# Causal attention on one core: the fourfold copy of v is dropped, and v is turned by products with the unit matrix

## The reference

```
t = t + attention(layer_norm(t))
Q = n @ W_Q;  K = n @ W_K;  V = n @ W_V        # n = layer_norm(t)
scores = Q K^T / sqrt(32), masked to key <= query
out = softmax(scores) V
```

## Time and profile before

| | us |
|---|---|
| median of three runs | 5225.98 |
| profiled execution | 5203.04 |
| its span in the trace | 5201.3 |

### The profile page before, as it was taken

The page is one execution under the profiler, slowest core; times in us unless marked ns, Lnnn a source line. Parts: engine busy times, 40 slices in busy tenths (PEclk is TensorE's granted clock), DMA queues, the critical chain, the costliest instruction groups (busy, mean ns, idle before and its releaser), DMA issues. The chain is left out here.

```text
span 5201.3 us, 102304 instructions
## 1 busy us (share of the span) xinstructions
PE 4473.6 (86%) x39002; PEld 2775.7 (53%) x39002; DVE 3218.9 (62%) x6562; ACT 2836.1 (55%) x5790; POOL 1475.1 (28%) x2257
## 2 busy tenths in 40 slices
PE   4888888886754899999999997679999999999955
PEld 2666666665322455555555554555555555555544
DVE  4777777776796466666666564336666666666532
ACT  2766676665654356555555554315555555655521
POOL 3111111111354333334243322023333243333100
PEclk8998999988877799999999998769999999999966
DMA  1100000000000000000000000000000000000003
GB/s 26 27 2 2 2 2 2 2 2 3 1 1 0 1 2 2 2 2 2 2 2 2 2 2 5 1 1 2 2 2 2 2 2 2 2 2 2 2 5 49
DMA packets 348174, 22.44 MB, mean 4 GB/s; under 512 B 346388, under 2 KB 347700, under 8 KB 347700
## 3 DMA queue, kind: packets, MB, share of 16 engines
q1 hardware_dynamic: 347700, 16.03, 4.2%
HBM read 7.88 MB, written 6.42 MB: 3 GB/s over the span
## 5 line engine op out<-in xcount | busy, mean ns | idle before, releaser
L551 DVE TENSOR_REDUCE L2a_mx<-L2a_r 128x1 f32<-128x512 f32 (+4 forms) x1344 | 771.0, 627 | 334.2 <-PE L2a_r L415 326.8
L551 DVE TENSOR_REDUCE L3a_mx<-L3a_r 128x1 f32<-128x512 f32 (+4 forms) x1344 | 770.8, 627 | 331.3 <-PE L3a_r L415 323.7
L415 PE MATMUL L2a_r<-L2a_vT,L2a_qT 32*128 32x512 f32 (+3 forms) x3488 | 885.5, 529 | 13.2 <-DVE L2a_mx L551 12.5
L415 PE MATMUL L3a_r<-L3a_vT,L3a_qT 32*128 32x512 f32 (+3 forms) x3488 | 881.8, 527 | 12.9 <-DVE L3a_mx L551 12.3
L514 ACT ACTIVATE L2a_e<-L2a_r 128x512 f32<-128x512 f32 (+3 forms) x1344 | 669.1, 569 | 266.8 <-PE L2a_r L394 263.3
L514 ACT ACTIVATE L3a_e<-L3a_r 128x512 f32<-128x512 f32 (+3 forms) x1344 | 669.0, 569 | 266.7 <-PE L3a_r L394 263.2
L394 PE MATMUL L2a_r<-L2a_qT,L2a_vT 32*128 32x512 f32 (+4 forms) x3488 | 772.4, 513 | 2.8 <-DMA L2a_qT<-L2a_nm 2.7
L394 PE MATMUL L3a_r<-L3a_qT,L3a_vT 32*128 32x512 f32 (+4 forms) x3488 | 770.8, 511 | 3.8 <-DMA L3a_qT<-L3a_nm 3.8
L415 PEld LDWEIGHTS L2a_r<-L2a_vT,L2a_qT 32*128 32x128 f32 x3488 | 387.4, 190 | 158.5 <-DVE L2a_mx L551 90.1
L415 PEld LDWEIGHTS L3a_r<-L3a_vT,L3a_qT 32*128 32x128 f32 x3488 | 385.8, 189 | 156.7 <-DVE L3a_mx L551 89.8
L1471 POOL TENSOR_SCALAR win_xw<-win_xr,win_rs,win_sh 32x343 f32<-32x343 f32 (+7 forms) x432 | 186.5, 446 | 937.0 <-DVE win_sh L1340 936.9
(11 more groups left out here) (376 smaller groups left out, 7573.8 us busy)
## 6 DMA issues: line engine op xcount, KB each, us to landing
L2a_qT<-L2a_nm SPq DMA_DIRECT2D x768, 0.5 KB, 2.0
L3a_qT<-L3a_nm SPq DMA_DIRECT2D x768, 0.5 KB, 2.0
T<-in_x SPq DMA_DIRECT2D x16, 384.0 KB, 3.8
out<-T SPq DMA_DIRECT2D x16, 384.0 KB, 4.0
win_mq<-win_nmt SPq DMA_DIRECT2D x256, 3.1 KB, 1.7
win_msk<-in_L_conv_pos_emb SPq DMA_DIRECT2D x49, 0.2 KB
L2a_qT<-L2a_nm SPq DMA_DIRECT2D x32, 0.2 KB, 1.8
L3a_qT<-L3a_nm SPq DMA_DIRECT2D x32, 0.2 KB, 1.8
```

The source lines that it names most:

```text
L415: return nc.tensor.matmul(bank_of(x)[:, o:o + c1 - c0], QT_[g0:g0 + C, img % 2, q0:q0 + P], VT[g0:g0 + C, img % 2, c0:c1], start=start, st ...
L551: return nc.vector.tensor_reduce(to, frm, AX.X, ALU.max)
```

## The change

`VR`, its memset, the item "vr" and the semaphore `vr_ready` are gone. The item vT now waits for `v_ready` and makes four products per tile: the weights are the 32 channels of the tile in `V`, the moving operand is the unit matrix, and product g writes partitions 32g to 32g + 31 of the bank. The due times of the vT items are moved within the image before. In the sorted list the seven vT items of an image were at the pv batches of slots 5, 15, 15, 26, 41, 50 and 60; now they are at 15, 26, 33, 41, 50, 50 and 60. Item v keeps its due time, and its rank is again the last.

```
-    RANK = {..., "out": 11, "vr": 12, "v": 13}
+    RANK = {..., "out": 11, "v": 12}
...
-            at = (img - 1) * PER + (4, 12, 20, 28, 38, 48, 58)[f]
+            at = (img - 1) * PER + (18, 24, 30, 38, 46, 54, 64)[f]
...
-        timed += [(vr - 19, ("res", img)), (vr - 7, ("rs", img)), (vr, ("vr", img)), (v, ("v", img))]
+        timed += [(vr - 19, ("res", img)), (vr - 7, ("rs", img)), (v, ("v", img))]
...
-        VR = sb("vr", [P, NT, QT, C])
...
-                nc.vector.memset(VR[:, :, :, 0:1], 1.0)
...
-                    elif kind == "vr":
+                    elif kind == "v":
                         img = x[1]
                         pool.wait_ge(root_ready, ROOT[("rs", img)] + 1)
-                        if img:
-                            pool.wait_ge(item_full, FILLED[("vT", img - 1, NJ - 1)] + 1)
-                        nc.gpsimd.tensor_tensor(
-                            VR[:, :, :, 1:C], RES[:, :, None, 1:C].to_broadcast([P, NT, QT, C - 1]),
-                            RSTD[:, img % 2][:, :, None, None].to_broadcast([P, NT, QT, C - 1]),
-                            ALU.mult).then_inc(vr_ready, 1)
-                    elif kind == "v":
-                        img = x[1]
                         if img > 1:
                             pool.wait_ge(pv_done, score_at(img - 1, 0))
...
                         if f == 0:
-                            pe.wait_ge(vr_ready, img + 1)
+                            pe.wait_ge(v_ready, img + 1)
                         for i in range(q_tiles(f)):
                             t = QT * f + i
                             r = rows(t)
-                            last = nc.tensor.transpose(bank_of(x)[:, i * P:i * P + r],
-                                                       VR[0:r, t].rearrange("p a c -> p (a c)"), k.ident[0:r, 0:r])
+                            for g in range(4):
+                                last = nc.tensor.matmul(bank_of(x)[g * C:(g + 1) * C, i * P:i * P + r],
+                                                        V[0:r, img % 2, t, :], k.ident[0:r, 0:r],
+                                                        start=True, stop=True)
```

More of the change, by code:

```diff
@@ L146, in causal_attention @@
             MAXES += [(img, j, x) for x in banks]
-    RANK = {"max": 1, "score": 0, "q": 2, "pv": 3, "acc": 4, "final": 5, "vT": 6, "mask": 7, "rs": 8, "ors": 9, "res": 10, "out": 11, "vr": 12, "v": 13}
+    RANK = {"max": 1, "score": 0, "q": 2, "pv": 3, "acc": 4, "final": 5, "vT": 6, "mask": 7, "rs": 8, "ors": 9, "res": 10, "out": 11, "v": 12}
     timed = [(n, ("score", n)) for n in range(NS)]
@@ L263, in _ @@
                 nc.vector.memset(O0[:], 0.0)
-        vr_ready, v_ready = sem("vr_ready"), sem("v_ready")
+        v_ready = sem("v_ready")
         stat_step, var_ready, log_ready, root_ready = sem("stat_step"), sem("var_ready"), sem("log_ready"), sem("root_ready")
```

## The result

The changed kernel takes 5405.36 us (median of four runs, 5390.51 to 5409.18) against 5222.56 us for the kernel before, run beside it (four runs, 5218.76 to 5230.42). The ratio is 1.0355, with a 95% interval of 1.0337 to 1.0373, so 183 us more. The forecast was 180 us more, 5406 us. The total fits better than its terms do; the experiments show that their errors cancel.

A forecast was written before the change was run, and what follows sets the result against it. TensorE was taken to bound the kernel. Products 67, wait for v 79, clock falls 44 and layer start -10 us summed to +180 on 5226, giving 5406 us, range 5325 to 5500.

The forecast's parts named there:

- What bounds the kernel: In pv phases TensorE sets the pace, busy 86% of the span; work added there delays everybody behind it.
- A: vT on TensorE, images 1 to 15 of both layers: products cost more than transposes, 67 us (32 to 224).
- D: Start of each layer: earlier first vT and no first-pv gap, against slower image 0 products; net -10 us in all.
- The factor of four: Rival on vT: transposes four times faster than float32 products, so products cost 273 us, in all 5612 us; chance 0.03.
- The rival of column tiles not side by side: On vT: a tile's products take 0.432 us, so products cost 224 us, in all 5563 us; chance 0.07.
- B: First vT of images from 2 on: TensorE waits 2.82 us for GpSimd's v in 28 places, 79 us.
- C: Behind the wait for v: TensorE's clock falls nearly each time, 28 x 1.56 = 44 us (0 to 73).
- the new due times: vT items move from slots 5 and 15 to 33 and 50, one starved phase to another; costed at nothing.
- more falls at block 0: With the vT gone from slot 5, the clock may fall at block 0 in the other images too, 23 us more.
- The rival on the other side: Seven banks between TensorE and VectorE/ScalarE hide added time and wait; only layer starts remain: 5207 us, chance 0.04.

The follow-up runs named there:

- doubled products: Changed kernel with v ranked before final, each tile's four products issued twice, against the kernel before: 5414.55 us, ratio 1.0380.
- products alone: Kernel before, keeping copy and old due times, each transpose replaced by four products with the unit matrix: 5306.12 us, ratio 1.0174.
- v ahead of final: Changed kernel with only v's rank edited, so GpSimd writes v before adding block 0's result: 5261.94 us, 1.0088 of the kernel before.
- the kernel with the clock held: Changed kernel in which TensorE fills its wait for v with twelve bf16 products: 5340.7 us, 1.0225 of the kernel before.
- the late copy: Kernel before with copy and v of image 1 due three slots later: 5206.71 us, ratio 0.9979; with new vT due times too, 5189.07 us, 0.9945.
- the new times alone: Kernel before with the new due times of vT and nothing else: 5200.73 us against 5211.81, ratio 0.9977.

## Why the prediction was right

**What bounds the kernel: right.** Each microsecond added to TensorE in a pv phase came back in the time: products, doubled products and the wait all did (the wait 2.72 of its 2.75 us, the second set of products 5.35 us per image).

**A, the products: right in kind, too small.** The term was 67 us, and the 4.5 us per layer for image 0 in D belong to it, 76 together. The products alone cost 91 us (79 to 102 by the interval). The step that was off is the duration of a group, 0.86 us by the first eight records of a pv. A single group takes 1.02 us and two together 1.88, so the places of an image take 6.2 us in the changed kernel against 3.2 with transposes, 3.0 us more where 2.2 was forecast; the distances without falls say 3.15 for the two shown (93.93 against 90.77) and 3.0 in the mean. The price of more records was right: a second set of 32 makes a single group 0.87 us longer, 0.109 us per four records, and 5.35 us per image. So the missing time belongs to the group and not to the records, and I had no row for that. The factor of four in the Trainium skill ("TensorE: Matmul & The Clock Gate", section Terms) asked for 273 us. This case's trace does not agree with it: products and transposes of an image stand at 6.2 to 3.2 us, a factor of 1.9. The rival of column tiles not side by side (224 us) did not come true either.

**B, the wait for v: right.** The chain read off appeared unchanged. TensorE was idle for 2.75 us in 27 of the 28 places and for 3.10 in one; the forecast of 2.82 was counted from where the vT would have started without the wait. In the distances the wait is worth 2.72 us, and 28 x 2.72 = 76 us against 79.

**C, the clock: the mechanism right, the size too small.** I expected a fall nearly each time and took its price from a fall of 3 us, 1.56 us. That price was right for such a fall (with v ahead of final, an image with one and the next are together 1.50 us longer). But a fall came in all 28 places, and 24 of them lasted 7 us, as behind the one gap of 3 us in the earlier trace rows; that was the nearer row, and I used it only as a bound (2.6 us). Measured are 2.33 us for a fall of 7 us and about 1.4 for one of 3.5, so 24 x 2.33 + 4 x 1.4 = 62 us against 44. The ratios of the kernel with the clock held give 68, within some 13. B and C together: 138 us by the distances and 139 by v ahead of final, 123 forecast.

**D, the start: the sign right, the gain larger.** From products alone (164.3 and 167.2 us) to the kernel with v ahead (150.3 and 151.8) the start shortens by 14.7 us per layer, of which the new times make some 2. Forecast were 3.9 + 5.6 = 9.5. The 5.6 of the gap at the first pv is confirmed by the late copy, 11 us for two layers. Up to the first score, L2a gained 3.8 us, just the earlier first vT. L3a gained 6.9: in it, the kernel with products alone stayed at half clock throughout, while with v ahead the clock rose for 3.4 us, as it did with products alone in L2a. What is left, some 2 us per layer behind the first score, isn't settled.

**Costed at nothing and not nothing:** the new due times, 12 us gained. I had warned of more falls at block 0 with the vT gone from slot 5. The opposite happened: 17 before, one in the changed kernel, two with the new times alone.

**The sum.** Forecast: 76 + 123 - 19 + 0 = 180 us. Measured: 91 for the products, 139 for wait and clock, -12 for the times, and -33 for what is left between products plus times and the kernel with v ahead (0.0174 - 0.0023 - 0.0088 = 0.0063), which stands for the start. That gives 185 us; it must come near the whole, since the last term is what remains. What it shows is the terms: products and wait with clock were 15 and 16 us too small, the gains of start and times 14 and 12. They cancelled; 5406 against 5405.4 us owes something to luck, the range and the sign do not.

**The rival on the other side**, that the ring of banks covers TensorE's extra work, needed VectorE to hold unread banks at the end of the final. It held none before, and was idle for 5.85 us after.

## What to carry to other kernels

When work leaves an idle engine, ask what it produced and when, and from which item the consumer will now take it. Here the copy was early and its substitute late, behind another item on the same queue, and a tie in the sorted order decided 139 us. Where a list orders all engines, read for each engine what stands directly ahead of the new producer and follow that back to the consumer itself: GpSimd's addition needed TensorE's final, and TensorE then stood still for it. And price an idle gap of TensorE with the clock behind it; in this kernel nearly half of what the wait cost was the clock's.

## What the runs showed of the hardware that I had not expected

- **A start at half clock can be avoided by filler.** In the kernel before, TensorE is idle for 17 us at the start of a layer, then runs some 40 us of products at 1.2 GHz (0.50). With 60 filler products of 512 columns in that idle time the clock reads 1.00 (2.4 GHz) from the first vT on, though the work behind the filler is the same. The way from the beginning of the copy of image 0 to the first score shrinks from 43.9 to 26.8 us, and both layers together gain 26 us or more over the same kernel without filler.
- **Filler ahead of the start was enough.** Four more products ahead of each later vT brought no gain (0.9895 against 0.9887), and the first score came 4.7 us later with them (31.6 us). No kernel has these alone, without the filler in the wait.
- **The same holds in small.** Twelve filler products in a wait of 2.75 us saved 2.33 us per image, where the clock had fallen for 7 us, without shortening the wait.
- **Float32 products of 32 columns of weights and 128 moving columns** run four side by side on the column tiles at 0.109 us per four records. A group of 32 records takes 1.02 us by itself. Turning the 25 tiles of an image by products takes 6.2 us of TensorE against 3.2 by transposes, about twice as much.
